# Hybrid scan layer with routed experts: feed-forward, router and experts in one part, expert tiles gathered by a list made on chip

## The reference

```python
x = x + _L0_attn_ref(_layernorm(x), ...)   # gated scan (mamba2), then silu(h @ gate_w) * (h @ up_w) @ down_w
x = x + _L0_ffn_ref(_layernorm(x), Wr, Wg, Wu, Wd)

# _L0_ffn_ref: 8 experts of width 352, 2 per row
probs = softmax(x @ Wr)
topk_w, topk_idx = top_k(probs, 2);  topk_w = topk_w / sum(topk_w)
y_e = (silu(x @ Wg[e]) * (x @ Wu[e])) @ Wd[e]
out = sum over the row's two experts of topk_w * y_e
```

## Time and profile before

| | |
|---|---|
| runs | 1609.54, 1609.52, 1608.76 us, median 1609.52 |
| the profiled execution | 1608.9 us, span 1607.2 us |
| mean granted TensorE clock | 0.957 |
| busy share: TensorE, VectorE, ScalarE, POOL | 89%, 48%, 28%, 27% |
| DMA | 147.12 MB, mean 92 GB/s |

### The profile page before, as it was taken

How to read it: one execution, slowest core, us unless ns; L and a number is a source line. 1 busy time by engine, 2 the same in 40 slices (tenths; PEclk the granted TensorE clock), 3 DMA queues, 4 the chain that set the end, 5 groups by cost and what they waited for, 6 DMA issues and landing times. The chain is left out here.

```text
span 1607.2 us, 20104 instructions
## 1 busy us (share of the span) xinstructions
PE 1432.8 (89%) x6651; PEld 1035.5 (64%) x6652; DVE 776.9 (48%) x1357; ACT 446.9 (28%) x924; POOL 441.4 (27%) x486
## 2 busy tenths in 40 slices
PE   5799999799999969999999999999720899999996
PEld 4677778466666648888888888888410555555553
DVE  5868778699999852433333333334544122121211
ACT  3444444545555531222111221111210111111110
POOL 1412111277777661110101101010116122222222
PEclk9899999899999989999999999999865899999998
DMA  8123125432233229100100001000595222222220
GB/s 185 53 78 120 66 79 164 158 130 95 99 113 111 93 63 369 67 27 14 39 13 26 26 13 39 0 1 0 190 369 188 73 74 89 81 87 90 80 86 15
DMA packets 92867, 147.12 MB, mean 92 GB/s; under 512 B 29182, under 2 KB 45566, under 8 KB 92800
## 3 DMA queue, kind: packets, MB, share of 16 engines
q1 hardware_dynamic: 79424, 119.92, 22.7%
q0 software_dynamic: 8800, 25.21, 4.6%
q10 hardware_dynamic: 4576, 1.13, 0.3%
HBM read 91.63 MB, written 58.27 MB: 93 GB/s over the span
## 5 line engine op out<-in xcount | busy, mean ns | idle before, releaser
L1372 PE MATMUL ff_bank<-ff_hT_hi,ff_w_hi 128*128 128x512 f32 x512 | 202.2, 395 | 5.3 <-POOL ff_w_lo L1278 5.3
L1372 PE MATMUL ff_bank<-ff_hT_hi,ff_w_lo 128*128 128x512 f32 x512 | 204.4, 399 | 0.0
L1372 PE MATMUL ff_bank<-ff_hT_lo,ff_w_hi 128*128 128x512 f32 x512 | 202.6, 396 | 0.0
L1814 PE MATMUL ex_bank<-w_gu,xT 128*128 x624 | 192.8, 462 | 1.4 <-ACT xT L1745 0.8
L1338 DVE TENSOR_TENSOR ff_prod<-ff_prod,ff_bank 128x512 f32<-128x512 f32 x64 | 44.1, 688 | 267.2 <-PE ff_bank L1372 253.3
L1278 POOL TENSOR_TENSOR ff_w_lo<-ff_stage,ff_w_hi 128x1024 fp32r<-128x1024 f32 x24 | 57.5, 2400 | 408.2 <-ACT ff_w_hi L1325 408.1
L1814 PEld LDWEIGHTS ex_bank<-w_gu,xT 128*128 128x128 f32 x624 | 116.3, 191 | 60.6 <-issue 3.3
L1784 DVE SCALAR_TENSOR_TENSOR result_rows<-ex_bank,xs,result_rows 128x512 f32<-128x512 f32 x39 | 29.3, 751 | 255.9 <-DMA result_rows<-out_dram,xs 253.3
L599 PE MATMUL pj_bank<-hT_hi,w_in_hi 128*128 128x512 f32 x336 | 137.4, 409 | 10.6 <-DVE zst L525 4.6
L507 DVE SCALAR_TENSOR_TENSOR conv_acc<-raw,conv_w,conv_acc 128x512 f32<-128x512 f32 x144 | 113.9, 791 | 47.0 <-ACT raw L326 37.0
L599 PE MATMUL pj_bank<-hT_lo,w_in_hi 128*128 128x512 f32 x336 | 135.7, 404 | 0.0
(11 more groups left out here) (238 smaller groups left out, 2414.6 us busy)
## 6 DMA issues: line engine op xcount, KB each, us to landing
cv_rows<-cst SPq DMA_DIRECT2D x12, 1024.0 KB, 4.2
cv<-cv_rows SPq DMA_DIRECT2D x16, 768.0 KB, 4.3
sorted_rows<-blank SPq DMA_DIRECT2D x1, 10023.0 KB, 43.7
xs<-sorted_rows SPq DMA_DIRECT2D x39, 257.0 KB, 2.7
zs_rows<-zst SPq DMA_DIRECT2D x8, 1024.0 KB, 6.3
zs<-zs_rows SPq DMA_DIRECT2D x16, 512.0 KB, 5.3
w_gu<-in_L_ffn_Wg_dram SPq DMA_DIRECT2D x8, 704.0 KB, 10.7
w_gu<-in_L_ffn_Wu_dram SPq DMA_DIRECT2D x8, 704.0 KB, 11.6
```

The lines of the kernel that those rows point to most:

```text
L1372: mm = eng.matmul(ps, w[a], x[b], start=first and i == 0, stop=last and i == 2)
L1814: mm = eng.matmul(ps[:, 0:EI], xT[v % 2][:, k, :], w_gu[:, i, bass.ds(e * KD + k, 1), :].rearrange("p a n -> p (a n)"), start=(k == 0), st ...
```

## The change

`feed_forward` and `experts` become one function `finish` with one block, so the two barriers between them go. The parts of it:

SP no longer fills `sorted`. Expert weights are laid out expert by expert in `wx`, over buffers of the feed-forward part; each part is loaded as soon as its place is free: experts 0, 1 and most of 2 before the last step, the rest after. Output rows are stored group by group, and so are the normalised rows `xn`, to DRAM.

```diff
-            eng.wait_ge(s["blanked"], 2)
-            eng.dma_start(dr["sorted"].rearrange("(t p) n -> p t n", p=P),
-                          blank[:, :].unsqueeze(1).broadcast_to([P, SORT_TILES, SD])).then_inc(s["cleared"], 16)
+            eng.dma_start(wr[:, :, :], ins["L0_ffn_Wr"].rearrange("(k p) e -> p k e", p=P)).then_inc(s["wr_dma"], 16)
...
+            load_expert(0, (0, 1, 2))
+            load_expert(1, (0,))
+            eng.wait_ge(s["down"], LAST * NR * TPR + CR)
+            load_expert(1, (1, 2))
+            load_expert(2, (0, 1))
+            store_out(0)
+            store_xn(0)
+            store_out(1)
+            store_xn(1)
+            eng.wait_ge(s["up_ps"], NB * NR * NI)
+            load_expert(5, (2,))
+            load_expert(6, (0, 1, 2))
+            load_expert(7, (0, 1, 2))
+            store_out(2)
+            store_xn(2)
+            store_out(3)
+            eng.wait_ge(s["down"], NB * NR * TPR + CR)
+            load_expert(2, (2,))
+            load_expert(3, (0, 1, 2))
+            load_expert(4, (0, 1, 2))
+            load_expert(5, (0, 1))
```

```diff
             def body(b, k):
                 following(width, b, k)
+                if isinstance(b, int) and b == LAST and k % NR:
+                    normed(k % NR - 1)
+                if isinstance(b, int) and b == LAST and k % NR == NR - 1:
+                    eng.wait_ge(s["up_ps"], NB * NR * NI)
+                    eng.wait_ge(s["logits"], 1)
+                    step(eng.tensor_copy(wsum[:, :], logit_ps[:, TILES * E:TILES * E + E]))
...
+            step(eng.tensor_tensor(sc[:, :, :], per_tile(mv[:, :, 0]), per_expert(wsum[:, :]), ALU.mult))
+            eng.wait_ge(s["logits"], TILES + 1)
...
+            normed(NR - 1)
...
+            eng.wait_ge(s["out_dma"], 16 * NR)
+            NS = 2 * TILES
+            step(eng.tensor_tensor(oj[:, :, 1, :], iota_q[:, 1, 0:SORT_TILES].unsqueeze(1).broadcast_to([P, NS, SORT_TILES]),
+                                   slot[:, 1, :].unsqueeze(2).broadcast_to([P, NS, SORT_TILES]), ALU.is_equal))
+            assert done[0] == R_EQJ, done[0]
+            for n in range(0, NS, 8):
+                eng.tensor_tensor(onehot[:, n:n + 8, :], iota_q[:, 1, :].unsqueeze(1).broadcast_to([P, 8, P]),
+                                  slot[:, 2, n:n + 8].unsqueeze(2).broadcast_to([P, 8, P]), ALU.is_equal)\
+                   .then_inc(s["onehot"], 1)
+                if n == 0:
+                    eng.wait_ge(s["ojid"], 1)
+                    eng.tensor_tensor(oj[:, :, 1, :], oj[:, :, 1, :],
+                                      wk[:, :, :].rearrange("p k t -> p (k t)").unsqueeze(2)
+                                      .broadcast_to([P, NS, SORT_TILES]), ALU.mult).then_inc(s["onehot"], 1)
+            step(eng.tensor_tensor(cmp_t[:, :, :], ends[:, 1, :].unsqueeze(1).broadcast_to([P, SORT_TILES, E]),
+                                   iota_q[:, 1, 0:SORT_TILES].unsqueeze(2).broadcast_to([P, SORT_TILES, E]), ALU.is_le))
+            step(eng.tensor_reduce(te_f[:, :], cmp_t[:, :, :], AX_X, ALU.add))
+            step(eng.tensor_scalar(te_f[:, :], te_f[:, :], float(E - 1), None, ALU.min))
+            step(eng.tensor_copy(tile_expert[:, :], te_f[0:1, :]))
+            eng.wait_ge(s["table"], 1)
+            eng.tensor_scalar(idx[:, :], table_ps[:, 0:SORT_TILES], float(ROWS), None, ALU.add).then_inc(s["ids"], 1)
+            eng.tensor_copy(wt[:, :], table_ps[:, SORT_TILES:2 * SORT_TILES]).then_inc(s["ids"], 1)
```

```diff
                 following(width, b, k)
+                if isinstance(b, int) and b == LAST and k % NR == NR - 1:
+                    router_sums()
                 out(b, k)
...
+            def turn_rows(t):
+
+                eng.wait_ge(s["add"], added(t // TPR, t % TPR))
+                ge(eng, s["xT"], t - 2)
+                for k in range(KD):
+                    last = eng.transpose(turn_ps[t % 3][:, k * P:(k + 1) * P], acc[:, t, k * P:(k + 1) * P], ident[:, :])
+                last.then_inc(s["rowT"], 1)
+
+            def logits(t):
+
+                eng.wait_ge(s["xT"], t + 1)
+                eng.wait_ge(s["route"], 1)
+                for k in range(KD):
+                    last = eng.matmul(logit_ps[:, t * E:(t + 1) * E], xT_r[:, t % 3, k, :], wr[:, k, :], start=(k == 0),
+                                      stop=(k == KD - 1))
+                last.then_inc(s["logits"], 1)
+
+            for t in range(TILES + 2):
+                if t < TILES:
+                    turn_rows(t)
+                if t >= 2:
+                    logits(t - 2)
+
+            eng.wait_ge(s["const"], 11)
+            eng.wait_ge(s["route"], R_HOT)
+            flat = hot[:, :, :].rearrange("p t e -> p (t e)")
+            eng.matmul(count_ps[:, 0:P], strict[:, :], flat, start=True, stop=True)
+            eng.matmul(count_ps[:, P:2 * P], ones[:, :], flat, start=True, stop=True).then_inc(s["counts"], 1)
+            NS = 2 * TILES
+            for n in range(NS):
+                if n % 8 == 0:
+                    eng.wait_ge(s["onehot"], n // 8 + 2)
+                last = eng.matmul(table_ps[:, 0:2 * SORT_TILES], onehot[:, n, :], oj[:, n, :, :].rearrange("p v j -> p (v j)"),
+                                  start=(n == 0), stop=(n == NS - 1))
+            last.then_inc(s["table"], 1)
...
+            turn_x(0)
+            eng.wait_ge(s["wx_dma"], 16 * 4 * E)
+            eng.wait_ge(s["route"], R_TE)
+            wide(0)
+            turn_x(1)
+            for j in range(SORT_TILES):
+                turn_width(j)
+                if j + 1 < SORT_TILES:
+                    wide(j + 1)
+                if j + 2 < SORT_TILES:
+                    turn_x(j + 2)
```

```diff
+            eng.wait_ge(s["route"], R_EQJ)
+            eng.wait_ge(s["const"], 11)
+            eng.tensor_tensor(oj[:, :, 0, :].rearrange("p (k t) j -> p k t j", k=2), oj[:, :, 1, :].rearrange("p (k t) j -> p k t j", k=2),
+                              rowm[:, 1, :].unsqueeze(1).unsqueeze(3).broadcast_to([P, 2, TILES, SORT_TILES]), ALU.mult)\
+               .then_inc(s["ojid"], 1)
...
+            def at(j):
+                return bass.IndirectOffsetOnAxis(ap=idx[:, j:j + 1], axis=0)
+
+            def gather(j):
+                if j >= UN:
+                    eng.wait_ge(s["xT_ps"], j - UN + 1)
+                    eng.wait_ge(s["sum"], j - UN + 1)
+                eng.indirect_dma_start(out=xs[j % UN][:, :], out_offset=None, in_=dr["xn"], in_offset=at(j),
+                                       bounds_check=ROWS - 1, oob_is_err=False).then_inc(xs_s[j % UN], 16)
+
+            gather(0)
+            gather(1)
+            eng.wait_ge(s["out_dma"], 16 * NR)
+            for j in range(SORT_TILES):
+                ge(eng, s["put"], 16 * j)
+                eng.indirect_dma_start(out=rows[:, :], out_offset=None, in_=out_d, in_offset=at(j),
+                                       bounds_check=ROWS - 1, oob_is_err=False).then_inc(s["got"], 16)
+                if j + 2 < SORT_TILES:
+                    gather(j + 2)
+                eng.wait_ge(s["sum"], j + 1)
+                eng.indirect_dma_start(out=out_d, out_offset=at(j), in_=rows[:, :], in_offset=None,
+                                       bounds_check=ROWS - 1, oob_is_err=False).then_inc(s["put"], 16)
+            eng.wait_ge(s["put"], 16 * SORT_TILES)
 
```

Removed, among the rest:

```diff
-                for n in range(2 * TILES):
-                    i, k = n // 2, n % 2
-                    eng.wait_ge(s["again"], 3 * n + 3)
-                    eng.indirect_dma_start(out=dr["sorted"][:, :],
-                                           out_offset=bass.IndirectOffsetOnAxis(
-                                               ap=slot[:, k * TILES + i:k * TILES + i + 1], axis=0),
-                                           in_=xm[n % 4][:, :], in_offset=None).then_inc(scat[n % 4], 16)
-                for i in range(4):
...
-                for n in range(2 * TILES):
-                    i, k = n // 2, n % 2
-                    if n >= 4:
-                        eng.wait_ge(scat[n % 4], 16 * (n // 4))
-                    normed(i, n % 4).then_inc(s["again"], 1)
-                    eng.tensor_copy(xm[n % 4][:, D:D + 1], weight[:, k, i:i + 1]).then_inc(s["again"], 1)
-                    eng.tensor_copy(xm[n % 4][:, D + 1:SD].bitcast(mybir.dt.int32), row_no[:, i:i + 1])\
-                       .then_inc(s["again"], 1)
...
-                def body(j, v):
-                    if not beyond(j, 2):
-                        eng.wait_ge(s["through"], j + 1)
-                        load(j + 2, (v + 2) % UN)
...
-                def body(j, v):
-                    number = bass.IndirectOffsetOnAxis(ap=xs[v][:, D + 1:SD].bitcast(U32), axis=0)
-                    eng.wait_ge(xs_s[v], (j - v) * 4 + 16)
-                    eng.sem_inc(s["passed"], 1)
-                    eng.indirect_dma_start(out=rows[:, :], out_offset=None, in_=out_d, in_offset=number,
```

(15 more changed lines are left out.)

664 lines of the change are left out of this document (288 added, 376 removed).

## The result

The changed kernel takes **1801.0 us** (median of 4 runs, 1796.5 to 1804.0) against 1609.1 of before: ratio 1.119, 95% interval 1.117 to 1.121. The forecast was 1549 us, in a range of 1530 to 1578, with a chance of 0.03 for slower. The profiled execution has a span of 1802.0 us against 1607.2, so there are 194.8 us to account for.

What follows compares the result with a forecast made beforehand. Bound: the round trip of output rows in the expert loop (gather, addition, scatter), 8.81 us a tile, TensorE 0.7 behind. Span 1607.2 - 47.5 (change-over) - 13 (loop) = 1546.7, plus 1.7 and rounding: 1549 us, range 1530 to 1578.

Steps and rivals of the forecast that it cites:

- POOL's 3.2 us of room: Expert loop: the third indirect transfer's 1.9 us on POOL fits between output gather issue and addition's end, so costs nothing.
- rival B: Expert loop: third transfer sharing POOL and software queue lengthens the round trip by 0.5 to 1.9 us a tile; chance 0.14.
- (a): Change-over: router column sums ahead of the last down products, 8 weight loads with tiny moving operands, 1.5 us.
- (b): Change-over: transposes and logits of 16 tiles, bound by weight loads, 1.6 us a tile, 27.3 us; bounds 22 to 33.
- (f): Change-over: 64 table passes of 78 columns, 16 at 0.3 and 48 at 0.125, 10.8 us; bounds 7 and 21.
- (c): Change-over: 15 VectorE steps on 128x128 up to the one-hot sum, starting 0.32 apart, 5.2 us.
- (d): Change-over: VectorE's normalisations, running sums, ends, places and comparison over 1248 elements, together 9.8 us.
- (e): Change-over: POOL multiplies 1248 elements, then VectorE's weight product, together 4.6 us.
- (g): Change-over: reading the list, start of the gather and the gather itself, 4.6 us.
- Rival C: Change-over late through slow small products, the table at low clock or late weights: 16 to 25 us, about 1568; chance 0.16.
- the cover: Change-over: expert weight transfers end near 1175, first product needs them near 1203, 28 us of cover, so no wait.
- rival A: Expert loop: gather lands in 2.8, round trip falls below TensorE's pace, 8.08 to 8.15 a tile, 1537 us; chance 0.15.

Runs made afterwards that it cites:

- e4: Changed kernel with input rows by plain loads of consecutive rows in SP's queue, two indirect transfers a tile on POOL; 1562.6 us, ratio 0.972.
- e7: Changed kernel with four input gathers ahead of the loop and none in it, inputs of later tiles left out; 1561.7 us.
- e1: Changed kernel with POOL sending the input gather of tile j+3 instead of j+2, three gathers ahead of the loop; 1559.1 us, ratio 0.971.
- e8: Changed kernel with five unused 512-column products on TensorE ahead of the transposes that wait for the input gather; 1744.8 us, ratio 1.085.
- e12: The same kernel as e1 without edit, run beside e11 on the same chip; 1559.8 us, ratio 0.969.
- e10: e9 plus 512-column filler products during routing, four ahead of the counts and thirteen behind them on an expert weight buffer; 1561.7 us.
- e9: e1 plus one unused 256-column product behind each tile's logits in the change-over; 1558.9 us, ratio 0.971.
- e11: As e10, but twelve fillers behind the counts, reading a buffer that is ready earlier; 1557.7 us, ratio 0.969.

## Why the prediction was wrong

**The loop: wrong, and it is nearly the whole miss.** The span is 255.3 us over the forecast 1546.7: the loop is 231.6 longer where it was to be 13 shorter, 244.6 in all; the change-over adds 12.1, and the feed-forward part ended 1.4 earlier. The step that failed is the sentence on POOL's 3.2 us of room with "It is hidden". It was true of the *issue*: e4 and e7 have no third transfer on POOL in the loop and are no faster than e1. It was silent on the *landing*. The prediction noted that the gather of tile j+2 stands between output gather j and scatter j, and in the changed kernel TensorE has `turn_x(j + 2)` ahead of `down(j)`, the order it had before; the two were not put together. What waits for gather j+2 are the transposes, and behind them stands what scatter j needs, while gather j+2 itself is issued only after scatter j-1 landed.

The kernel before has the same order on TensorE and loads "two tiles ahead" as well. But there the load of tile j+2 waits for `through` to reach j+1, and `through` starts at 2: it is released by scatter j-2, not j-1. In its timeline SP's load at 1404.54 is the one of tile j+4 behind scatter j (start 1401.57, rows 5); it lands 2.7 us later, near 1407.2, and TensorE transposes it here (first weight load at 1408.81), with 1.6 us to spare and no wait for a DMA:

```profile
1409.10 0.60 PE L1805 MATMUL ex_bank<-ident,xs 128*128 128x128 f32 x4
```

Moving the transfer into POOL's program put it one scatter, 8.8 us, later. e1 gives back just this tile. The circle could have been summed beforehand, nearly to its length; with the values of the runs after where rows of before lack one: scatter 2.76 and 0.99 to the output gather, 1.0 and 0.3 of issue, input gather 3.4, transposes 0.66, down products 2.85, addition 0.76, 0.88 to the scatter: 13.6 us a tile. e8, at the full clock, has 13.67 over the first 34 scatters and 13.31 over all. The rest of the 14.88, 1.57, is the clock, which TensorE's wait costs; its size no row of before gave, but the earlier trace rows showed the clock at 0.50 in a pause. The chance of 0.03 for slower was attached to rival B, so no branch of the prediction had this circle.

**Rival B** had the right sign and the wrong mechanism: 0.5 to 1.9 us a tile from a shared queue. Measured for a shared queue: nothing that can be told (over the first 34 scatters 8.64 in e1, 8.65 in e7; 8.82 in e4, which has the third transfer in SP's queue). The rule of the Trainium skill behind it (DMA: Bandwidth & Descriptors, SWDGE vs HWDGE vs iDMA: one software queue) decided nothing here.

**With the circle open half of the term comes out.** Over the first 34 scatters e1 has 8.64 us a tile, before 8.81, and 8.46 were forecast: 0.17 less instead of 0.35, or 6 us instead of 12. The gather stayed at 3.4 instead of 3.3, and one scatter took 4.35. First transpose to end is 349.0 in e1 (1557.6 - 1208.6), 9.1 less than before against 13 forecast, but the nearness is in part luck: 4.9 of the 9.1 lie behind the start of the last scatter (4.0 us to the end of the span against 8.9 before), which the forecast did not have, and the last four tiles took 2.0 more, not 1 less.

**The change-over: inside its bounds, 12 us above its value** (75.9 against 63.8; bounds 50 to 85). In e1 and e7 it was near 70, and e12 shows that such a difference needs no edit. Term by term in the changed kernel:

- (a) router sums 0.9 us ahead of the last down products; 1.5 forecast. They lie ahead of the stretch of 75.9 and not in it, so the like of the 75.9 in the forecast is 62.3.
- (b) from the first transpose (1136.6) to VectorE's first step (1173.9) 37.3; 27.3 forecast, bounds 22 to 33. This is the term mis-sized, beyond its own bounds; the sum stayed inside because the others did not err by as much. At the full clock a tile takes 1.28 in e1 (transposes start at 1141.87, 1143.16, 1144.44), under my 1.6; at 0.50 it takes 2.45. I had priced the products by records at the full clock and thought of the clock only in (f), though the earlier trace rows had 0.86 for the like stage of before.
- (c) 4.7; 5.2 forecast. (d) and (e) together 14.6; 14.4 forecast. The small steps start 0.32 apart, as taken from the earlier trace rows.
- (f) 14.05; 10.8 forecast: all 64 passes at the low clock, 0.22 each, and not the first 16 alone. (g) 5.0; 4.6 forecast. Rival C, the small products and the table slower than taken, was thus right in kind; it is worth 12 us of the 255.

**The weights** were no wait: ahead of the first gate/up product of the changed kernel, at 1214.2, stand 0.78 us for ACT. Its transfers ended between 1176 and 1178, where the DMA share falls from 0.98 to 0.18, against 1175 forecast, so the cover was some 36 us and not 28. In e10 the last piece landed later, at 1181.3.

**A figure of rival A** does not come out: 1537 less the 13.8 us from 63.8 down to 50 is 1523, not 1527. Nothing else was built on it.

The span of e1 is 49.6 us under that of before: 1.0 later end of the feed-forward part, 41.5 less change-over (69.8), 9.1 less from the first expert transpose to the end. The forecast had 60.5; of the 11 that lack, 6 lack in the change-over, 4 from the first expert transpose on, and 1 is the later end.

## What to carry to other kernels

When a transfer moves to another engine's program, write down for it three things: after which event it is issued, who waits for its landing, and what stands behind that waiter in its queue. If what stands behind leads back to the event, the time of the whole circle is the new period, whatever room each engine has. "Two tiles ahead" is no lead until it is said ahead of what; count it from the event that releases the issue, and give one tile more than the circle needs. Of a stage of small products, ask at which clock it will run before pricing it.

## What the runs showed of the hardware

- A pause of TensorE was paid twice here: waits near 5 us in each tile of the loop (14.88 us a tile) brought its granted clock to 0.83, and useless products in the pause (e8) brought it back to 1.00 and made the kernel 56 us faster.
- TensorE can be busy without a gap and still be granted the lower level: 0.50 to 0.51 over 30 us of loads with 8 and 128 moving columns. With one product of 256 columns a tile more (e9) it was 1.00 through the whole stage. When it falls differs between executions of the same kernel: near 1150 us in e1, near 1141 in e12, worth 6 us.
- After a pause of 3.6 us (e11) the list products ran at the low level, 13.6 us for 64 passes; the same followed 14 us of products without a pause at the full one in 7.3 (e10). Behind a pause of 0.9 us (e10, e11) the counts took 0.49 for two passes, instead of 0.77 behind a pause of 4.9 in the changed kernel.
- A float32 product of 128x512 is recorded as two passes, which follow each other 0.43 us apart at the full clock (e8: ten in 4.45, each record 0.59 long).
- An indirect gather of 256 KB takes 3.4 us with another one beside it (e1) or without (e7), a scatter 2.8 in both; in the last five tiles they take 2.1 to 2.7.
